# 500-column products that nothing reads, placed between TensorE's own in two edge stages of a graph network kernel

## What is computed

```python
# layer 0
e   = relu(edge_attr @ ee_w1 + ee_b1) @ ee_w2 + ee_b2      # 100000 edges, 64 -> 256 -> 256
agg = segment_sum(h[src] + e, dst)                          # per node
h   = mlp((1 + eps) * h + agg)                              # 256 -> 1024 -> 1024 -> 256, layer norms
x   = x + relu(layernorm(h0 + h))
# layer 1: attention over the edges, 8 heads of 32
e     = leaky_relu(h_src[src] + h_trg[dst]); exp_e = exp(e - max)
out   = segment_sum(h_prime[src] * exp_e / denom[dst], dst)
x     = x + out
```

## Time and profile before

| | us |
|---|---|
| median of three executions | 4217.17 |
| the profiled execution, its own time | 4245.11 |
| its span, first to last instruction | 4243.3 |
| TensorE busy | 2741.7 (65%) |
| TensorE weight loads | 2350.9 (55%) |
| VectorE busy | 2441.3 (58%) |
| GpSimd busy | 2001.3 (47%) |
| ScalarE busy | 1418.1 (33%) |
| mean granted TensorE clock | 0.814 of full speed |

### The profile page before, as it was taken

The page is one execution under the profiler, slowest core; times in us unless marked ns, Lnnn a source line. Parts: engine busy times, 40 slices in busy tenths (PEclk is TensorE's granted clock), DMA queues, the critical chain, the costliest instruction groups (busy, mean ns, idle before and its releaser), DMA issues. The chain is left out here.

```text
span 4243.3 us, 86741 instructions
## 1 busy us (share of the span) xinstructions
PE 2741.7 (65%) x25602; PEld 2350.9 (55%) x25603; DVE 2441.3 (58%) x5647; ACT 1418.1 (33%) x3617; POOL 2001.3 (47%) x2147
## 2 busy tenths in 40 slices
PE   0056565666666665899999999836554666666663
PEld 0045555555545455888888888824443444444442
DVE  3545555555555553566666666645545555566566
ACT  1522222222222232677777777611100111111110
POOL 0245554555555552333333333335545555565554
PEclk9977787788777777999999999956667777777766
DMA  5333333333333332011100110034434444444443
GB/s 158 123 103 103 109 108 102 111 106 111 106 108 105 104 111 66 20 30 30 30 30 30 30 30 30 28 98 123 120 104 118 112 130 129 127 133 132 127 128 102
DMA packets 203584, 393.32 MB, mean 93 GB/s; under 512 B 45288, under 2 KB 98028, under 8 KB 202900
## 3 DMA queue, kind: packets, MB, share of 16 engines
q0 software_dynamic: 75552, 209.66, 18.1%
q1 hardware_dynamic: 125750, 182.11, 14.1%
q10 hardware_dynamic: 2222, 0.87, 0.1%
HBM read 360.28 MB, written 32.20 MB: 92 GB/s over the span
## 5 line engine op out<-in xcount | busy, mean ns | idle before, releaser
L522 POOL DMA_INDIRECT rows<-tab_scratch,idx x784 | 768.8, 981 | 675.4 <-POOLq L520 438.9
L1474 POOL DMA_INDIRECT a_rows<-tab_scratch,a_srcs x784 | 772.1, 985 | 614.3 <-PEq L1579 399.5
L1539 PE MATMUL sum_ps<-feat,a_hot 128*125 128x264 f32 x1960 | 709.8, 527 | 421.3 <-PEq L1578 287.2
L1539 PEld LDWEIGHTS sum_ps<-feat,a_hot 128*125 128x125 f32 x1960 | 485.1, 258 | 551.5 <-issue 440.6
L948 PE MATMUL z_ps<-ah,w2h 128*128 128x125 f16 x3200 | 543.3, 220 | 0.8 <-PEq L1020 0.6
L948 PE MATMUL z_ps<-ah,w2l 128*128 128x125 f16 x3200 | 543.2, 218 | 0.0
L948 PE MATMUL z_ps<-al,w2h 128*128 128x125 f16 x3200 | 543.2, 217 | 0.0
L549 ACT ACTIVATE rh<-mlp_ps 128x1024 f16<-128x1024 f32 x196 | 200.7, 1024 | 907.2 <-ACTq L548 729.6
L569 PE MATMUL sum_ps<-rows,hot 128*125 128x256 f16 x980 | 325.8, 332 | 272.8 <-issue 127.6
L562 PE MATMUL mlp_ps<-ewa,eab 128*128 128x256 f16 x788 | 230.7, 318 | 403.0 <-PEq L558 343.8
L1486 ACT ACTIVATE feat<-d 128x32 f32<-128x32 f32 x196 | 45.0, 229 | 1230.7 <-ACTq L1485 833.4
(11 more groups left out here) (214 smaller groups left out, 6455.6 us busy)
## 6 DMA issues: line engine op xcount, KB each, us to landing
ea<-edge_t SPq DMA_DIRECT2D x394, 128.0 KB
dstb<-dst_flat SPq DMA_DIRECT2D x196, 256.0 KB
rows<-tab_scratch,idx POOLq DMA_INDIRECT x784
a_rows<-tab_scratch,a_srcs POOLq DMA_INDIRECT x784
tab_scratch<-prow SPq DMA_DIRECT2D x50, 128.9 KB
acc<-x SPq DMA_DIRECT2D x5, 1250.0 KB
h_scratch<-h SPq DMA_DIRECT2D x10, 625.0 KB
tab_scratch<-tb SPq DMA_DIRECT2D x10, 625.0 KB
```

The lines of the kernel that those rows point to most:

```text
L522: pool.indirect_dma_start(rows[:, s, k, :], None, dram["tab0"], bass.IndirectOffsetOnAxis(ap=idx[:, s, k:k + 1], axis=0),).then_inc(rows_r ...
L1474: pool.indirect_dma_start(rows[:, b % RING, k, :], None, dram["tab1"], bass.IndirectOffsetOnAxis(ap=srcs[:, c:c + 1], axis=0),).then_inc(r ...
L1539: ins = pe.matmul(out[:], hot[:, h, k, :], feat[:, row, k, :], start=(k == 0), stop=(k == CB - 1))
```

## The change

A helper `kept_busy(n)` issues n products of a 128 x 125 weight tile (`iota16`) with 500 columns (`iota16` repeated four times) into a PSUM tile of their own, and nothing reads that tile. In `edges0` three stand between `edge_mlp` and the waits ahead of `sums`, one each takes the place of the one-column products that signal `r_free` and `rows_free`, and two follow at the end of the batch. In `edges1` three stand between `sums` and `prepared`, one takes the place of the one-column product ahead of `ht_done`, and two follow.

```diff
@@ edges0
-        used_ps = m.ps("used_ps", [1, 1])
+        busy_ps = m.ps("busy_ps", [TN, CB * TN])
...
+            def kept_busy(n):
+
+                for _ in range(n):
+                    ins = pe.matmul(busy_ps[:], iota16[:], iota16[:].unsqueeze(1).broadcast_to([P, CB, TN]), start=True, stop=True)
+                return ins
...
                     edge_mlp(1 - s)
+                    kept_busy(3)
                     lo, end = tiles[u]
...
-                    pe.matmul(used_ps[:], ewa[:, 0:1], ewa[:, 0:1], start=True, stop=True).then_inc(r_free, 1)
-                    pe.matmul(used_ps[:], ewa[:, 0:1], ewa[:, 0:1], start=True, stop=True).then_inc(rows_free, 1)
+                    kept_busy(1).then_inc(r_free, 1)
+                    kept_busy(1).then_inc(rows_free, 1)
+                    kept_busy(2)
@@ edges1
-        used_ps = m.ps("a_used_ps", [1, 1])
+        busy_ps = m.ps("a_busy_ps", [TN, CB * TN])
...
                 other_targets(ht_ps[s], lo, end)
-                pe.matmul(used_ps[:], ident[:, 0:1], ident[:, 0:1], start=True, stop=True).then_inc(ht_done, 1)
+                kept_busy(1).then_inc(ht_done, 1)
+                kept_busy(2)
...
                     sums(sum_ps[s], u, u).then_inc(sum_done, 1)
+                    kept_busy(3)
                     if has(i, u, 3):
                         prepared(1 - s, (u + 3) % RING, *tiles[u + 4])
```

## The result

| | before | after |
|---|---|---|
| median, us | 4216.24 (4 runs, 4206.21 to 4219.63) | 4358.18 (4 runs, 4339.40 to 4368.69) |
| ratio, 95% interval | | 1.0331 [1.0305, 1.0357] |
| profiled execution, its own time, us | 4245.11 | 4339.40 |
| mean granted TensorE clock | 0.814 | 0.872 |

The kernel is 3.3% slower, by 142 us, although its TensorE clock is higher.

A forecast was written before the change was run, and what follows sets the result against it. No single engine bounds the edge stages; a ring of dependences with TensorE in it does. First stage 49 x (3.0 - 2.1) = +44 us, second 0, onto 4217 gives 4261 us, +1.0%; range 4120 to 4360 us.

The forecast's parts named there:

- No effect on the second stage: Second edge stage: six products a batch, 1.3 us, cost nothing under VectorE's cover; length stays 1372 us within 15.
- some 0.88: First edge stage: granted TensorE clock rising from 0.78 to about 0.88 would show the clock part right.
- How much goes away? ... I take half: First edge stage: of 4.3 us a round lost to the low clock, half, 2.1 us, comes back.
- 147 - 103 = +44 us: First edge stage: products' cost, 3.0 us a round, less clock gain, 2.1 us, over 49 rounds: +44 us.
- has no product in it at all: First edge stage: the 2.49 us wait ahead of the extra sums gets none of the new products.
- I charge the extra-tile batch 0.65 us and of the three ordinary ones half: First edge stage: products cost 0.65 us in the extra-tile batch, 2.3 us in three ordinary ones, 3.0 us a round.
- mostly for `r_free`: ScalarE at L548: its 730 us of waiting was said to be mostly for this signal from TensorE.
- the add at 980.16: VectorE, first edge stage: idle for 5.13 us though its sums were finished, so a wait TensorE cannot shorten.
- Rival 2: First edge stage: products run slow and on the path, +3.9 us a round, +190 us, 4407 us; chance 0.10.
- Its second part: TensorE's unexplained "issue" idle time, 197 us, grows by a fifth with its longer program: 39 us.
- Rival 1: First edge stage: clock held, over 3.0 of 4.3 us a round back on the path; 4125 to 4146 us; chance 0.36.
- Rival 3: Waits of 5 us that belong to no sum set the round; no change, 4205 to 4230 us; chance 0.16.

The follow-up runs named there:

- narrow_again: Kernel before plus seven products of 8 columns, not 500, a batch in the first edge stage only: 4335.80 us against 4238.15, ratio 1.0228.
- longer10: Kernel before plus ten semaphore instructions a batch in TensorE's first-stage loop, no new products: 4312.95 us against 4212.46, ratio 1.0228.
- sets 1, 3 and 4: Groups of follow-up runs, each compared with the unchanged kernel before of its own group, which took 4164.03, 4238.15 and 4212.46 us.
- sets 2 and 5: Groups of follow-up runs, each compared with the unchanged kernel before of its own group, which took 3543.92 and 3542.32 us.
- half_width: Kernel before plus seven products of 250 columns, not 500, a batch in the first edge stage only: 4396.09 us against 4238.15, ratio 1.0346.
- longer20: Kernel before plus twenty semaphore instructions a batch in TensorE's first-stage loop, no new products: 3820.12 us against 3542.32, ratio 1.0773.
- shorter4: Kernel before with four semaphore instructions fewer a batch in TensorE's first-stage loop, no new products: 3540.69 us against 3542.32, ratio 1.0001.

## Why the prediction was right and wrong

It said slower, 4261 us, +44; it is slower by 142. The wide range, 4120 to 4360, just reaches it; the forecast's own range of 4232 to 4320 does not.

**Right.** Seven products a batch, not nine. 0.21 us each. An ordinary batch of TensorE's at 4.1 us (4.3 was said). No effect on the second stage: 1372 us, and there even twelve a batch cost nothing, in the set with the short stages; that VectorE's 5.27 us from batch to batch and the gathers cover them is the likely reason and was not tested. That the clock rises and yet the kernel doesn't get faster: 0.85 was measured where some 0.88 was said.

**Wrong, the gain: this is the step that failed.** The step "How much goes away? ... I take half", 103 us, and its silent sequel, that what goes away is on the path. TensorE got 68 us back, 74 by the mean records, and only 14 us of them where VectorE and ScalarE stood idle. Where the sum had 147 - 103 = +44 us, the account has 100 of new products alone less 14 of gain, and 14 more of VectorE's and ScalarE's work: about the 96 us by which the stage grew. (The other 48 us up to 142 are in no pair of profiles.) The cold products were read from the batch with an extra tile, where all is on the path; but the ones that were warmed are the MLP's and those of the main tile's sums, and the sixteen extra sums, which stay cold, have no product ahead of them in their wait. The prediction had noted just this ("has no product in it at all") and drew no number from it.

**Not settled, the place of the cost.** "I charge the extra-tile batch 0.65 us and of the three ordinary ones half", 2.3 us. Cut behind a batch's sums, the three ordinary batches take 2.8 us a round more and the one with the extra tile 0.8 less, where the sum had 0.65 - 2.1, that is 1.45 less. Cut from MLP to MLP, it is 0.15 and 1.8 us more. What the rows do show is one piece: behind an extra tile the MLP is late already, and the four products ahead of it take nearly 0.4 us each (1016.78 above). The total, 147 us charged against 100 of new products alone, was not too low. But it was worked out from the products' width, and `narrow_again` loses 98 us with products of almost no width: that the common idle times can grow, as they did there, had no place in the sum.

**Wrong, two readings of rows.** ScalarE's wait of 730 us is not "mostly for `r_free`" but for `mlp_done`. And the add at 980.16 did wait for TensorE: the record of the sums that it takes ends at 971.96, and its wait for `sum_done` at 979.96, another of the late signals.

**Rival 2** ("slow and on the path") came nearest in size, +190 us: the row at 1016.78 shows such products, and `narrow_again` says that they are not the whole. Its second part, 39 us for a longer program, was tested by itself and stays undecided: the "issue" idle time ahead of L575 is 72 us where it was 128, but all the idle time there grew by 18 us, one packet of instructions more came, and `longer10` paid no more than its instructions hold the queue. The Trainium skill, "Runtime: NRT & Kernel Launch", in "Instruction fetch mechanics", speaks of a forced fetch after a branch whose target isn't held. The rows of the instruction queue do not show one in this loop.

**Rival 1** failed at its own condition, that over 3.0 us of the 4.3 a round come back on the path: 68 us are 1.4 us a round, and those on the path 0.3. Rival 3, no change, is out by the time itself. The Trainium skill, "TensorE: Matmul & The Clock Gate", in "Why this matters for your kernels", advises to leave no long idle gaps between bursts of matmuls. The trace agrees that work put there raises the granted clock (0.78 to 0.85 and 0.72 to 0.83), and shows in the same rows that it can be worth nothing, or cost.

**What stays open.** Where the long common idle times come from, some 260 us of the stage in sets 1, 3 and 4 and about 50 in sets 2 and 5, for the same program. They are mostly waits for signals of TensorE that come late. In the kernel before three quarters of the late `sum_done` come over 0.7 us after the end of the last gather, that is behind a run of gathers, which follow each other in 0.3 us, as at 1011.38; but in the short stage GpSimd gathers all the time and no signal is late, and no experiment changed the gathers. Why the common idle times grew in `narrow_again` and `half_width` (328 and 355 us), and so how seven small products come to cost 98 us. Whether a longer program costs anything beyond its instructions' own time: the two kernels that would have told how it scales, `longer20` and `shorter4`, ran in the set whose stage was short. No version clearly beat the kernel before: twelve products a batch in the second stage alone gave 0.9978 [0.9969, 0.9988], in one of the two kinds of sets only, and six gave 1.0017 [0.9997, 1.0038] in the other.

## What to carry to other kernels

A cold TensorE costs only what of its cold time nothing else covers. Before putting work in to warm it, work out that part (TensorE busy, the others idle), and of it only what can be reached ahead of the wait; here 14 us came back where a total of 209 had been counted. Filler in the same queue ahead of late work can be paid at the low clock, 0.4 us a product in the row at 1016.78, and even filler of almost no width was not free in the long stage. A wait's label names the last instruction of the queue; which semaphore held it has to be read from the waits one by one. A split of the loss over batches is worth nothing until it has been made with a second way of cutting. And a granted clock that rises, 0.814 to 0.872, is no sign of a gain: look at the length of the stage.

## What was unexpected of the hardware

- The same program took 4164 to 4238 us in three sets and 3542 to 3544 us in two; sets 1, 4 and 5 were on the same chip. All the difference is in the two edge stages with their gathers: the first took 1444 and 1010 us, the second 1372 and about 1110.
- In the first stage of the long condition a third of TensorE's `sum_done` signals reached VectorE over 1.5 us after the recorded end of the product, up to 11.4 us (62 of 196 in the kernel before); in the short one none did.
- A semaphore instruction in TensorE's queue has a record of 51 ns, but ten in a row start 151 ns apart; ten in a batch cost 100 us.
- Products of 8 columns do not hold the clock: 0.74 with seven of them in a batch, 0.83 with seven of 500 columns.
